# Moving two kinds of loads in SyncE's program of a one-core Mamba, attention and experts kernel

## The reference

```python
# 1. two Mamba layers, 512 inner channels d, 64 states s (h: batch, d, s)
u, z = split(x @ in_w.T);  u = silu(causal_conv4(u))
dt, Bm, C = split(u @ xp_w.T);  dt = softplus(dt @ dtw.T + dtb);  A = -exp(A_log)
def step(h, inp):                       # over 256 tokens
    u_t, dt_t, B_t, C_t = inp
    h = h * exp(dt_t[:, :, None] * A) + (dt_t * u_t)[:, :, None] * B_t[:, None, :]
    return h, einsum('bds,bs->bd', h, C_t)
y = (scan(step) + u * D_skip) * silu(z);  out = y @ out_w.T
# 2. cross attention: softmax((x Wq + bq)(ctx Wk)^T / 16) (ctx Wv + bv) Wo + bo
# 3. mixture of 8 experts, top 2 of 8 by gate_probs, hidden width 1024
h = relu(x @ w1[e].T + b1[e]);  out = sum over the top 2 of weight * (h @ w2[e].T + b2[e])
```

## Time and profile before

| | |
|---|---|
| median of 3 runs | 3627.11 us (3620.34 to 3629.55) |
| the profiled execution | 3629.55 us |
| its span (first to last instruction) | 3627.8 us |
| VectorE busy | 3292.5 us, 91% |
| GpSimd, TensorE, ScalarE busy | 75%, 74%, 74% |
| granted TensorE clock, mean | 0.869 |

### The profile page before, as it was taken

One profiled execution on the slowest core, in us unless ns is written; L12 is line 12 of the kernel. 1 busy time (PEld: TensorE's weight loads), 2 busy tenths in 40 slices (PEclk: granted clock), 3 DMA queues, 4 the chain that ended last, 5 costly groups with the idle time before them and its releaser, 6 DMA issues.

```text
span 3627.8 us, 50146 instructions
## 1 busy us (share of the span) xinstructions
PE 2687.7 (74%) x16828; PEld 2279.6 (63%) x16828; DVE 3292.5 (91%) x3308; ACT 2678.4 (74%) x6210; POOL 2713.3 (75%) x1335
## 2 busy tenths in 40 slices
PE   5667676767667677788877777787777768788776
PEld 3555565656556566677666666766666657677665
DVE  4999999999999999999999999999999999999510
ACT  6868777786868678786887768787787768877422
POOL 5878788877878788786888778787888878867401
PEclk7878788888878899998999788999998789899888
DMA  2231111111111133323221132323221123234275
GB/s 93 83 130 59 41 50 42 47 42 44 45 53 42 40 104 99 109 78 124 97 98 63 40 115 91 123 89 96 100 96 59 46 96 102 100 108 148 92 264 173
DMA packets 148358, 319.58 MB, mean 88 GB/s; under 512 B 25451, under 2 KB 41844, under 8 KB 147461
## 3 DMA queue, kind: packets, MB, share of 16 engines
q1 hardware_dynamic: 144146, 305.60, 25.4%
q0 software_dynamic: 3072, 8.39, 0.7%
q10 hardware_dynamic: 882, 2.38, 0.2%
HBM read 286.42 MB, written 29.88 MB: 87 GB/s over the span
## 4 chain that ended last, share of the span: by engine, by line
DVE 43%; issue 22%; POOL 12%; PE 12%; ACT 10%; DMA 1%; SPq 0%; POOLq 0%; DVEq 0%
DVE h L1112 26%; DVE psX L1102 13%; POOL hC L872 9%; ACT dA L1080 4%; PE psG L1322 3%; PE psY L1370 2%; PE psX L1354 2%; ACT xs L1055 1%; PE psX L1322 1%; PE psG L1398 1%; PE psX L1398 1%; POOL dtu L811 1%; PE psG L1486 1%; POOL dt L806 1%; POOL scratch L788 1%
## 5 line engine op out<-in xcount | busy, mean ns | idle before, releaser
L872 POOL TENSOR_TENSOR hC<-h,cb 128x1024 f32<-128x1024 f32 x1024 | 2410.9, 2367 | 674.6 <-DVE h L1112 665.2
L1112 DVE TENSOR_TENSOR_SCAN h<-dA,psX 128x512 f32<-128x512 f32 x2048 | 2365.1, 1205 | 47.7 <-PE psX L1354 22.0
L1080 ACT ACTIVATE dA<-dt,negA 128x255 f32<-128x255 f32 x4096 | 1722.0, 500 | 368.2 <-DVE h L1112 365.4
L1370 PE MATMUL psY<-ident,hC 128*128 128x128 f32 x8192 | 1255.3, 304 | 40.1 <-DVE gT L1126 37.1
L1370 PEld LDWEIGHTS psY<-ident,hC 128*128 128x128 f32 x8192 | 1095.7, 160 | 84.7 <-DVE gT L1126 41.4
L1102 DVE TENSOR_TENSOR psX<-dtu,psX 128x1024 f32<-128x1024 f32 x692 | 835.7, 1208 | 71.0 <-POOL dtu L811 39.3
L1354 PE MATMUL psX<-ident,xs 128*128 128x128 f32 x2656 | 433.6, 317 | 347.8 <-DVE h L1112 245.9
L1354 PEld LDWEIGHTS psX<-ident,xs 128*128 128x128 f32 x2656 | 354.9, 163 | 430.6 <-issue 274.4
L1055 ACT ACTIVATE xs<-dtuT,bT 128x512 f32<-128x512 f32 x664 | 440.9, 716 | 0.1
L1345 PE MATMUL psX<-bparts,sel 96*128 96x256 bf16 x692 | 210.4, 304 | 268.8 <-DVE h L1112 260.4
L1345 PEld LDWEIGHTS psX<-bparts,sel 96*128 96x128 bf16 x692 | 71.1, 103 | 391.6 <-DVE h L1112 365.7
(11 more groups left out here) (211 smaller groups left out, 1881.5 us busy)
## 6 DMA issues: line engine op xcount, KB each, us to landing
cb<-c_dram SPq DMA_DIRECT2D x256, 512.0 KB, 3.8
w_up<-in_w_exp SPq DMA_DIRECT2D x201, 256.0 KB, 2.8
w_down<-in_w_exp SPq DMA_DIRECT2D x201, 256.0 KB, 2.9
dA<-in_w_exp SPq DMA_DIRECT2D x39, 256.0 KB, 3.9
h<-in_w_exp SPq DMA_DIRECT2D x39, 256.0 KB, 4.3
x_slots<-got SPq DMA_DIRECT2D x16, 512.0 KB, 5.4
xg<-x_slots SPq DMA_DIRECT2D x60, 128.0 KB, 2.8
y_slots<-yg SPq DMA_DIRECT2D x60, 128.0 KB, 3.0
```

Of the source, the lines that this page charges most:

```text
L872: eng.tensor_tensor(hC[i % NHC][:, :, :], h[i % NH][:, :, :], cw.to_broadcast([P, KI, L]), ALU.mult).then_inc(times_c, 1)
L1080: made = eng.activation(dA[j % NA][:, c, 1:L], dt[n % 2][:, c, 1:L], ACT.Exp, scale=negA[:, JOBS[n][0], c, s:s + 1])
L1112: eng.tensor_tensor_scan(h[i % NH][:, 2 * f:2 * f + 2, :].rearrange("p c t -> p (c t)"), dA[i % NA][:, 2 * f:2 * f + 2, :].rearrange("p c ...
L1370: made = eng.matmul(psY[:, tc, c * P:(c + 1) * P], hC[i % NHC][:, c, tc * P:(tc + 1) * P], ident[:, :], start=s == 0 and c == 0, stop=Fals ...
```

## The change

SyncE's program alone is changed, in two places. The load of an input row is issued at piece `z`, part 0, of the job that reads it, no longer at `c_copy` of the job of layer 0 before it. The load of a group of C rows is issued at the head of step 4m+3 for group m+2, no longer at the head of step 4m+5 (which is 4(m+1)+1) for the same group. Its wait is the same, for the multiplication of step 4m+3. So it now stands ahead of SyncE's pieces of steps 4m+3 and 4m+4, and behind them before.

```diff
             def small_work(pieces):
                 for name, n, part in pieces:
-                    if name == "c_copy":
+                    if name == "z" and part == 0 and n > 0 and JOBS[n][0] == 0:
+                        load_row(JOBS[n][1])
+                    elif name == "c_copy":
                         ...
                         eng.dma_start(c_dram[n % 2], cdt[0:S, :]).then_inc(c_out, 16)
-                        if JOBS[n][0] == 0 and JOBS[n][1] + 1 < ROWS:
-                            load_row(JOBS[n][1] + 1)
                     ...
             for i in range(STEPS):
-                if i % CG == 1 and i > CG and i // CG + 1 < STEPS // CG:
-                    load_c(i // CG + 1)
+                if i % CG == CG - 1 and i // CG + 2 < STEPS // CG:
+                    load_c(i // CG + 2)
                 if S // 2 <= i and i % 2 == 0 and (i - S // 2) // 2 < CLEARS:
                     clear((i - S // 2) // 2)
                 small_work(plan.beside[i])
```

## The result

The changed kernel takes 3652.09 us (median of 5 runs, 3648.28 to 3660.00) against 3627.11 us (5 runs, 3620.34 to 3630.88): 1.0077 times as long, with a 95% interval of 1.0061 to 1.0091. It is slower by 25 to 28 us. The forecast was 3641 us, slower by 14: the direction was right, the size only half of what came. Measured again on the chip of the later experiments the ratio was 1.0093 (1.0079 to 1.0106). (One slip in the text ahead: the load that now stands at step 520 is that of row 5, not 4. Nothing hangs on it.)

A forecast was written before the change was run, and what follows sets the result against it. VectorE's chain of scans was taken as the bound; late rows (7.4 us), weights (9.6) and other loads (1) made 18 us, less about a fifth +14, so 3641 us; likeliest case 3636 to 3647, with neighbours 3628 to 3655.

The forecast's parts named there:

- the earlier C loads give nothing: Line 872, reader of C rows, waited for no transfer, so asking for them earlier gains nothing.
- loads behind them inherit a wait for GpSimd: SyncE's queue: loads behind a C load wait for GpSimd's multiplication; those of half the steps lose up to 6.5 us.
- the six places: Input rows at steps 520, 776 and weights at 559, 815, 931, 991 land late, costing 7.4 and 9.6 us.
- Lateness: How long after TensorE wants it a load lands: 6.2 us at step 520, 4.7 us beside step 559.
- the neighbour's price: SyncE's queue: the 512 KB C load just ahead delays a 256 KB load's landing by 1.5 us.
- The landing behind a C load: A 256 KB load behind a C load lands 4.4 us after issue; lower bound 2.9 us, 2.8 for weights.
- One clause: Claimed pieces of steps 4m+5 and 4m+6 meet the wait as before, formerly at 4m+5's head with a value four lower.
- TensorE slows down: Rival: half clock behind the six new waits, some 2 us more each, 12 in all, 3653 us; chance 0.12 (including stalls adding up).
- the fifth taken off as given back: From the 18 us sum, about a fifth returns as VectorE's idle time waits on engines that caught up, leaving +14 us.
- the two rows: Input rows at steps 520 and 776, each 6.2 us late, cost VectorE 3.7 us each, together 7.4 us.
- the four weights: Weight loads at steps 559, 815, 931, 991 come late and cost VectorE 9.6 us together.
- the other fifteen late loads: Weights and token tiles elsewhere, 0.2 to 3.4 us late; slack swallows nearly all, 1 us counted.

The follow-up runs named there:

- e1: Against before: only the loads of C rows moved as in the change, input rows loaded where they were; 1.0081 times before.
- e2: Against before: only the input rows' loads moved to the piece that reads them, C loads where they were; 1.0003 times before.
- e4: Changed kernel with the C loads one step later (group m+1 at the head of step 4m); 1.0049 times before.
- e6: Before with input rows loaded at piece z and only the C loads at steps 519 and 775 moved two steps ahead; 1.0027 times before.
- e7: Before with input rows at piece z and only the C loads at steps 559, 815, 931, 991 moved two steps ahead; 1.0062 times before.
- e11: e6 with each of the two late rows' loads issued ahead of the C load, behind the same wait; 1.0026 times before.
- e9: e6 plus 36 transposes of the identity ahead of TensorE's waits in pieces z of steps 520 and 776; 1.0032 times before.
- e10: e7 plus 36 transposes of the identity ahead of TensorE's waits at steps 560, 816, 992 and 30 at 932; 1.0037 times before.
- e3: Changed kernel plus 36 transposes of the identity ahead of TensorE's five waits over 5 us; 1.0081 times before.

## Why the prediction was half the size

**Right.** The bound (VectorE's scans), that the earlier C loads give nothing, that loads behind them inherit a wait for GpSimd, the six places and their order: all of it stands in the trace and in e1, e2, e4, e6 and e7. Lateness was estimated well: at step 520 it was 6.2 us against 5.7 measured, at 559 4.7 against 5.1 (a wait of 5.28 us, of which 0.17 was there before). So was the neighbour's price: 1.5 us assumed, 1.2 measured at the row (e11). The landing behind a C load was 3.9 us for the rows and 4.4 to 4.7 for the weights at the other four places, where 4.4 was assumed. One clause is the wrong way round: formerly the value four lower stood ahead of the pieces of steps 4m+3 and 4m+4; ahead of those of 4m+5 and 4m+6 the wait is the same in both orders. The prices at the six places do not rest on it.

**The step that failed** is the sum's silence on the clock: the rival "TensorE slows down" was given 0.12 with the words that in the quiet stretch VectorE is as busy at 0.83. That argument was wrong: there a slower TensorE works into its slack; here the half clock sets in within the very wait that has used up the slack (at 1736.0 in a wait that ends at 1737.8), and products and fill stretch on VectorE's path. What the six places cost with TensorE kept busy is what the forecast had computed: 6.8 us for the two rows (e9), where it had 7.4, and 9.5 for the four weights (e10), where it had 9.6; all in one kernel 19.1 (e3), where it had 17. What they cost as they are is 10.7 and 16.2 (e6, e7), and 30.2 in the changed kernel. The clock's share at the places is thus 10.6 to 11.1 us, where the rival had 12. That its time, 3653, met the result is in part luck: it contains the fifth taken off as given back, which did not come, and in the second session the changed kernel stood 34 us over before, not 26.

**Mis-sized beside it.** The fifth that I took off as given back, some 4 us: from step 512 on the delay grows by 30.4 us, with 30.2 at the six places. What VectorE catches up is made up by new small stalls. And of the other fifteen late loads, counted at 1 us in all, two cost 2.4 and 2.1 us (steps 980 and 1019): waits of 2.8 and 3.1 us, then a granted clock of 0.56 and 0.74 in the next 6 us, under which TensorE's products reach VectorE's next fill too late.

**What stays open.** The clock's share is shown at the places, stall by stall. In the whole time it isn't: e10 is 9 us faster than e7, e9 no different from e6, and e3 no different from the changed kernel, while from step 512 on their traces are 1.8, 3.3 and 8.4 us shorter. Part of the share is lost again where the next spell of half clock falls, as at steps 532 and 788, and part of the scatter behind the loop goes with the clock there; what sets the moment of a spell, no run here shows. A trace is also one execution only: that of e9 took 3625 us, where nine executions of this kernel lie between 3623 and 3643 with a median of 3633, and that of e3 was the fastest of five.

## What to carry to other kernels

In a queue that runs in order, a wait is a property of everything behind it: before moving a load ahead "because it only gets earlier", look what its semaphore waits for and who stands behind. A row's load moved to its piece was free (e2), and late as soon as a wait was moved ahead of it too (e6), so test edits apart and together. And price a new stall of TensorE twice: by its lateness, and by what its next products take at half clock when the slack is already gone.

## What had not been expected of the hardware

- In the changed kernel's loop all five waits of TensorE for a transfer of 5.3 us or more were followed by a granted clock of 0.50 to 0.58 in the next 6 us; of four waits of 2.6 to 3.1 us one was followed by 1.00 and three by 0.56 to 0.74; of 15 waits of 0.6 to 2.3 us, 11 by 1.00. The mean over the execution stayed at 0.87. In e7 the three waits of 5.1, 5.4 and 5.4 us (steps 560, 816 and 992) were followed by 0.75, 0.50 and 0.71.
- 36 idle transposes (4.1 us) in such a wait kept the clock at 1.0 and shortened the stall behind it from 5.3 to 3.4 us (steps 522 and 778, e6 and e9), from 4.3 to 2.7 (562, e7 and e10). In e9 the half clock then came some 21 us later than in e6, and VectorE stood for 1.4 us there.
- A 256 KB load directly behind a 512 KB one lands 1.2 us later than ahead of it (3.9 against 2.7 us, e6 and e11). In the whole changed kernel 71 loads of 256 KB directly behind a C load landed in 4.2 us by the median, 338 others in 3.1, and the page's median for `w_up` rose:

```profile
w_up<-in_w_exp SPq DMA_DIRECT2D x201, 256.0 KB, 3.4
```

from 2.8 us before.
